# Transposes of keys, query and layer-norm output as interleaved 64-row halves in a decoder layer kernel

## The chip, the cores and the metric

The kernel runs on one core of one Trainium2 chip, in one launch. The metric is the device time of that launch in microseconds (us); lower is better.

## The reference: what is computed

One pre-norm decoder layer over 32 sequences of 128 tokens, width 512, all in fp32:

```
x = x + self_attention(layernorm(x))            # 16 heads of 32, rotary positions, causal
x = x + cross_attention(layernorm(x), ctx)      # 32 heads of 16, axial rotary positions; ctx is 128 x 256
x = x + ffn(layernorm(x))                       # gate and up 512 -> 1408, SiLU, down 1408 -> 512, integer weights
```

Only the two attentions are touched by the change. For each sequence they need queries, keys and values from the normalised input, and the heads' scores need queries and keys with the head dimension on the partitions, so each 128x512 query and key tile is transposed on TensorE before use. So are the normalised inputs (they are the stationary operand of the projections) and the softmax probabilities (they multiply the values).

## The kernel before, in words

Every engine has its own instruction stream, written out by hand, and they meet only in semaphores. The work is one loop over sequences, skewed: a call of `turn(sq, cq, nx, nz, oq)` does self-attention of sequence `sq`, cross-attention of `cq = sq - 1`, the first projections of `nx = sq + 1`, the layer norm of `nz = sq + 2` and the last projection of `oq = cq - 1`. `schedule` calls it for the first four turns with constants, then 27 times in a hardware loop, then once more; `last()` finishes the last sequences. In 30 of these turns both `sq` and `cq` exist. The feed-forward part follows. Each engine runs its part of `turn` in the order in which it is written; nothing else sets the order of the work.

There are eight PSUM banks: `S[0]` to `S[3]` hold scores and then the transposed probabilities; `PA`, `PB`, `PC` and `TC` serve all projections and transposes in rotation.

Names that the change and the prediction use:

- `transpose4` (L497) makes four 128x128 transposes of a 128x512 tile into one bank. It is used for the rotated query and key tiles (`rope_buf` in the profile: q1, k1 of self-attention, q2, k2 of cross-attention), for `z1` and `z2` (the two layer norms' outputs, `z` in the profile) and for the spread reciprocals (`rbc`).
- `transpose_prob` (L541 to L557) transposes 16 heads' probabilities as 32 transposes of 64 rows each. Rows 0 to 63 of one bank's heads alternate with rows 64 to 127 of another's, so two neighbours never write the same bank. The other halves follow after a wait on `cross_d`, which says that the first halves are complete. There are three such blocks in a turn: `"1"` for self-attention, `"2a"` and `"2b"` for the two halves of cross-attention.
- ScalarE copies the transposed query, keys and `z1` out of PSUM (`copy_q2`, `copy_q1`, `kT1` at L977, `z1T_high` at L867), ScalarE and VectorE share the copies of the transposed probabilities (`odd_copies` L936, `even_copies` L1105). Projections run in three passes of split operands, so VectorE also makes `z1T_l`, the remainder of `z1` (`z1T_low`, L1094).
- VectorE makes two products for each rotation (L1049, L1052), and GpSimd adds them (`rope_sum`, L399) into `RA[...]`; the semaphore `rot[...]` counts that.
- `normalise(1, ...)` on VectorE (L1028 to L1033) makes `z1` of `nz`.

In TensorE's `turn` the part that the change reaches is this, in order: project q2 and o2; transpose q2; `transpose_prob("1")`; values; scores 2a; attention 1; reciprocals; project q1 and o1; `transpose_prob("2a")`; transpose q1; keys k2; scores 2b; project k1; attention 2a; ten of twelve steps of v1 (L602); transpose k2; transpose k1; `transpose_prob("2b")`; the last two steps of v1; transpose z2; transpose z1 of `nz`; then the next turn's scores 1.

Of the kernel before, what the change touches and what calls it, by code (L numbers as in the profile page):

```python
# [15 lines left out]
P = 128  # L16
B = 32
# [121 lines left out]
def attention_phase(nc, fp32, fp32r, ALU, ACT, AX, x, ctx_in, pos, consts,  # L139
                    wq1, wk1, wv1, wo1, wq2, wkv2, wo2, bout, x2_dram, shared_f, shared, ident, mhalf_c, ffn):  # L140
    es = ExitStack()
    with es:
# [101 lines left out]
        cross_d = {n: sem(f"prob{n}T_first_quarters_done") for n in (1, 2)}  # L244
# [249 lines left out]
        def _(pe):  # L494
# [45 lines left out]

            def transpose_prob(u, q):  # L541
                k = kind(u)
                for swap in range(2):
                    for pair in range(2):
                        if swap == 0:
                            pe.wait_ge(p_r[k], G * nth(u, q) + 2 * pair + 2)
                        else:
                            pe.wait_ge(cross_d[k], 2 * nth(u, q) + pair + 1)
                        pe.sem_inc(gate, 1)
                        for i in range(G):  # L550
                            for half, rows in enumerate(HALVES):
                                c = 2 * pair + (half ^ swap)
                                last = nc.tensor.transpose(S[c][:, i * P + rows.start:i * P + rows.stop],  # L553
                                                           prob[rows, c, i, :], ident[rows, rows])
                        if swap == 0:
                            last.then_inc(cross_d[k], 1)
                        else:  # L557
                            last.then_inc(pT_d[k], 2)
# [33 lines left out]
            def transpose_z1(q, dst=PC):  # L592
                pe.wait_ge(z_r[1], q + 1)
                transpose4(dst, columns(z1)).then_inc(zT_d[1], 1)
# [17 lines left out]

            def project_k1(q):
                pe.wait_ge(rT_r["q1"], q + 1)
                project(PA, z1T_h, z1T_l, "k1", KT).then_inc(pj["k1"], 1)
# [12 lines left out]
            def turn(sq, cq, nx, nz, oq):  # L628
                has_s, has_c, has_n, has_o = sq is not None, cq is not None, nx is not None, oq is not None

                if is_first(nx):
                    first_projections()
                    return
# [20 lines left out]
                if has_c:  # L654
                    pe.wait_ge(zT_hi[2], cq + 1)
                    if has_n:
                        pe.wait_ge(zT_hi[1], nx + 1)
                        pe.wait_ge(zT_lo[1], nx + 1)
# [22 lines left out]
                if has_s:  # L681
                    pe.wait_ge(v1_r, sq + 1)
                    if is_first(sq):
                        pe.wait_ge(zT_hi[1], nx + 1)
                        pe.wait_ge(zT_lo[1], nx + 1)
# [16 lines left out]
                if has_n and has_c:  # L702
                    transpose_q1(nx)
# [10 lines left out]
                if has_c:  # L714
                    if has_o:
                        pe.wait_ge(x2_r, oq + 1)
# [6 lines left out]
                if has_s:  # L723
                    pe.wait_ge(rot["k2"], sq + 1)
                    if is_first(sq):
                        pe.wait_ge(riT_r[1], 1)
                    transpose4(TC, columns(RA["k2"])).then_inc(rT_d["k2"], 1)
                if has_n:
# [120 lines left out]

            pe.wait_ge(c_ready, 6)  # L850
            transpose_z1(0)
            schedule(turn, pe.Fori, last)
# [3 lines left out]
        def _(act):  # L856
# [8 lines left out]
            def z1T_high(q, src=PC):  # L865
# [847 lines left out]
```

## Time and profile before

| | us |
|---|---|
| three runs | 1692.16, 1687.82, 3995.81 (median 1692.16) |
| the profiled execution's own time | 1687.21 |
| its span | 1685.4 |
| TensorE busy | 1641.8 |
| VectorE busy | 1150.1 |
| ScalarE busy | 972.0 |
| GpSimd busy | 552.8 |
| one turn, from one transpose of q1 to the next | 35.15 |

The busy times are of one profiled execution, whose time is the second row. Engines overlap, so busy times don't add up; a busy TensorE counts a matmul that is under way even when its neighbour has begun, so how long a group takes is read from start to start of groups. "PE" is the matmul side of TensorE, "PEld" its weight loads. An arrow behind "idle before" names what ended the wait.

### The profile page before, as it was taken

The numbers are of one execution on the slowest core, as the hardware profiler recorded it, in microseconds if no ns is written. First come the engines' busy times: TensorE is split into PE (matmuls) and PEld (weight loads), VectorE is DVE, ScalarE is ACT, GpSimd is POOL, SyncE is SP. The second block draws the span as 40 slices with busy tenths as digits, with TensorE's granted clock in tenths as the row PEclk, the third lists the DMA queues.
The fourth block names the chain that finished last, engine by engine and source line by source line (L and its number), as shares of the span: only waits on it lengthen the run. The fifth ranks groups of instructions, "written<-read, shape, count | busy, mean of one in ns | idle before, by whom it ended". The sixth has DMA issues, their size and how long they took to land. (4 is left out here: it accounts for less than half of the span.)

```text
span 1685.4 us, 40585 instructions
## 1 busy us (share of the span) xinstructions
PE 1641.8 (97%) x14608; PEld 1285.4 (76%) x14608; DVE 1150.1 (68%) x2087; ACT 972.0 (58%) x3817; POOL 552.8 (33%) x535
## 2 busy tenths in 40 slices
PE   6899999999999999999999999998999999999997
PEld 4677777777777777777777777766888888888885
DVE  7777778777787777877778787777744344344332
ACT  6577777777777777777677776766522222222221
POOL 4444444444444444444444444431011011011011
PEclk9999999999999999999999999999999999999999
DMA  6011111101110011100111101021520120120110
GB/s 214 29 32 31 36 43 41 30 30 36 42 42 30 30 36 41 43 30 30 36 39 45 30 30 39 19 74 65 174 76 19 56 75 21 54 75 23 52 50 26
DMA packets 55097, 80.98 MB, mean 48 GB/s; under 512 B 4880, under 2 KB 25488, under 8 KB 55056
## 3 DMA queue, kind: packets, MB, share of 16 engines
q1 hardware_dynamic: 55056, 80.43, 14.6%
q8 instruction: 27, 0.44, 0.1%
q14 instruction: 14, 0.11, 0.0%
HBM read 63.63 MB, written 16.78 MB: 48 GB/s over the span
## 5 line engine op out<-in xcount | busy, mean ns | idle before, releaser
L877 ACT ACTIVATE prob<-bank,nmax 128x128 f32<-128x128 f32 x1536 | 541.3, 408 | 151.0 <-DVE nmax L1099 148.1
L877 ACT ACTIVATION_READ_ACCUMULATOR prob<-bank,nmax 128x1 f32 x1536 | 380.2, 248 | 0.0
L1099 DVE TENSOR_REDUCE nmax<-bank 128x4 f32<-128x512 f32 x376 | 233.5, 683 | 71.4 <-PE bank L536 70.7
L1505 PE MATMUL fbank<-shared,piece_hi 128*128 128x512 f32 x1152 | 280.3, 394 | 0.0
L1505 PEld LDWEIGHTS fbank<-shared,piece_hi 128*128 128x128 f32 x1152 | 215.8, 187 | 53.2
L399 POOL TENSOR_TENSOR rope_buf<-rope_buf 128x512 f32<-128x512 f32 x128 | 168.0, 1323 | 175.6 <-DVE rope_buf L1052 175.5
L1657 DVE SCALAR_TENSOR_TENSOR h<-fbank,su_c,sil 128x512 f32<-128x512 f32 x88 | 65.9, 749 | 198.4 <-PE fbank L1505 197.0
L1591 ACT ACTIVATE sil<-fbank,sg_c 128x512 f32<-128x512 f32 x88 | 60.6, 688 | 173.1 <-PE fbank L1505 172.0
L449 POOL TENSOR_TENSOR cn_l<-cn,cn_h 128x512 fp32r<-128x512 f32 x64 | 82.9, 1296 | 230.2 <-DVE cn L1091 230.2
L1597 ACT ACTIVATE h_h<-h 128x512 fp32r<-128x512 f32 x88 | 55.6, 632 | 175.0 <-DVE h L1657 175.0
L512 PE MATMUL bank<-shared,z1T_h 128*128 128x512 f32 x520 | 140.3, 411 | 4.3 <-ACT shared L860 2.6
L936 ACT ACTIVATE probT<-bank 128x512 f32<-128x512 f32 x186 | 101.1, 596 | 66.1 <-PE bank L553 66.1
L1105 DVE COPY probT<-bank 128x512 f32<-128x512 f32 x186 | 117.8, 675 | 29.2 <-PE bank L553 29.2
L1488 POOL TENSOR_TENSOR xr<-xr,ys 128x512 f32<-128x512 f32 x32 | 40.3, 1294 | 288.9 <-DVE ys L1677 288.9
L553 PEld LDWEIGHTS bank<-ident,prob 64*128 64x128 f32 x2976 | 111.7, 138 | 23.5 <-issue 22.4
L553 PE MATMUL bank<-ident,prob 64*128 64x64 f32 x2976 | 125.7, 229 | 0.5 <-ACT prob L877 0.5
L512 PEld LDWEIGHTS bank<-shared,z1T_h 128*128 128x128 f32 x520 | 93.7, 190 | 34.4 <-issue 12.9
L1520 PE MATMUL fbank<-piece_hi,h_h 128*128 128x512 f32 x288 | 115.3, 400 | 0.5 <-DVE h_l L1660 0.5
L1520 PE MATMUL fbank<-piece_hi,h_l 128*128 128x512 f32 x288 | 113.6, 395 | 0.0
L1660 DVE TENSOR_TENSOR h_l<-h,h_h 128x512 fp32r<-128x512 f32 x88 | 62.9, 714 | 61.5 <-ACT h_h L1597 61.5
L405 POOL TENSOR_TENSOR rbc<-rinv,one_c 128x512 f32<-128x512 f32 x64 | 66.6, 1041 | 76.7 <-DVE rinv L1114 56.6
L536 PE MATMUL bank<-kT,qT 32*128 32x256 f32 x1024 | 76.4, 404 | 5.1 <-DVE probT L1151 3.0
(171 smaller groups left out, 3127.4 us busy)
## 6 DMA issues: line engine op xcount, KB each, us to landing
xA<-in_x SPq DMA_DIRECT2D x32, 256.0 KB, 2.9
xB<-in_x SPq DMA_DIRECT2D x32, 256.0 KB, 2.8
x_scratch<-x SPq DMA_DIRECT2D x32, 256.0 KB, 2.0
shared_loaded<-x_scratch SPq DMA_DIRECT2D x8, 1024.0 KB, 7.8
xr<-x_scratch SPq DMA_DIRECT2D x8, 1024.0 KB, 5.6
out<-xr SPq DMA_DIRECT2D x8, 1024.0 KB, 4.3
cx<-in_ctx SPq DMA_DIRECT2D x32, 128.0 KB, 2.2
range_window<-in_wg SPq DMA_DIRECT2D x27, 112.0 KB, 2.0
```

Of the source, the lines that this page charges most:

```text
L399: pool.tensor_tensor(RA[n][:, :], RA[n][:, :], RB[n][:, :], ALU.add).then_inc(rot[n], 1)
L405: pool.tensor_tensor(tile[:, :, :], r[:, :].unsqueeze(2).to_broadcast([P, h, w]), one_c[:, :].unsqueeze(2).to_broadcast([P, h, w]), ALU.mu ...
L449: pool.tensor_tensor(cn_l[:, :, :], cn[:, :, :], cn_h[:, :, :], ALU.subtract).then_inc(cn_lo[n], 1)
L512: last = nc.tensor.matmul(dst[:, :], a[:, j, :], w[:, j, cols], start=(n == 0), stop=(n == 3 * k - 1))
L536: last = nc.tensor.matmul(S[g][:, 2 * P * i:2 * P * (i + 1)], qT2[rows, j, :], kT2[rows, j, :, :].rearrange("p e t -> p (e t)"), start=Tru ...
L553: last = nc.tensor.transpose(S[c][:, i * P + rows.start:i * P + rows.stop], prob[rows, c, i, :], ident[rows, rows])
L877: last = nc.scalar.activation(prob[:, c, i, :], S[c][:, i * P:(i + 1) * P], ACT.Exp, bias=nmax[:, c, i:i + 1], accum_out=rs[:, h:h + 1])
L936: nc.scalar.activation(probT[:, c, :, :].rearrange("p g t -> p (g t)"), S[c][:, :], ACT.Copy).then_inc(pTo_r[kind(u)], 1)
L1099: nc.vector.tensor_reduce(out=nmax[:, c, :], in_=S[c][:, :].rearrange("p (g k) -> p g k", g=G), op=ALU.max, axis=AX, negate=True).then_inc ...
L1105: nc.vector.tensor_copy(probT[:, c, :, :].rearrange("p g t -> p (g t)"), S[c][:, :]).then_inc(pTe_r[kind(u)], 1)
L1505: last = nc.tensor.matmul(dst[:, :], w[:, k, cols], z[:, k, :], start=(n == 0), stop=(n == len(passes) * KT - 1))
L1520: last = nc.tensor.matmul(DN[s][:, :], a[j % 2][:, tok], w[piece][:, j % 2, :], start=(j == 0 and n == 0), stop=(j == HT - 1 and n == len( ...
```

## The change: what it does

- **Keys.** k2 and k1 are transposed together as 64-row halves: rows 0 to 63 of k2 into `TC` alternate with rows 64 to 127 of k1 into `PA`; after that the first halves of the first two banks of `"2b"` probabilities; then, after a wait on the first halves of the keys, the other halves of both. The block waits for both `rot["k2"]` and `rot["k1"]` before it begins.
- **Second query and z1.** The transpose of the next input's `z1` leaves the end of the turn and is paired in the same way with q2, inside the block of `"1"` probabilities, one turn later in number (`nx` in place of `nz`). ScalarE's `z1T_high` moves behind `copy_q2`, VectorE's `z1T_low` moves behind `even_copies("1")`, and VectorE's `normalise(1, ...)`, which overwrites `z1`, moves behind the rotation of q1.
- **First query.** q1's two row halves go to two banks, 256 columns of `PA` and 256 of `PB`, as eight 64-row transposes with no second set; ScalarE copies it with two instructions of 128x256 in place of one of 128x512. The wait for `x2_r` (the residual sum that reads `PB`) comes forward with it.
- One semaphore, `halves_d`, replaces `cross_d`; a Python counter gives the value to wait for.

The core of the diff:

```diff
+            def halves_of_two(tiles, swap):
+                for j in range(KT):
+                    last = []
+                    for half, rows in enumerate(HALVES):
+                        dst, src = tiles[half ^ swap]
+                        last.append(nc.tensor.transpose(dst[:, j * P + rows.start:j * P + rows.stop],
+                                                        src[rows, j * P:(j + 1) * P], ident[rows, rows]))
+                return last
+            def transpose_keys_and_probs(sq, cq, nx):
+                keys = ((TC, RA["k2"]), (PA, RA["k1"]))
+                pe.wait_ge(rot["k2"], sq + 1)
...
+                pe.wait_ge(rot["k1"], nx + 1)
+                keys_ready = first_halves_of_two(keys)
+                if cq is not None:
+                    ready = [first_halves_of_probs("2b", cq, 0)]
+                k2, k1 = second_halves_of_two(keys, keys_ready)
...
+            def transpose_query_z1_and_probs(sq, cq, nx):
+                tiles = ((PA, RA["q2"]), (PC, z1))
+                pe.wait_ge(rot["q2"], cq + 1)
+                pe.wait_ge(v1_r, sq + 1)
+                pe.wait_ge(z_r[1], nx + 1)
+                tiles_ready = first_halves_of_two(tiles)
+                ready = [first_halves_of_probs("1", sq, 0)]
+                q2, z = second_halves_of_two(tiles, tiles_ready)
...
+            def transpose_q1_halves(q):
+                pe.wait_ge(rot["q1"], q + 1)
+                pe.sem_inc(gate, 1)
+                for j in range(KT):
+                    for half, rows in enumerate(HALVES):
+                        last = nc.tensor.transpose((PA, PB)[half][:, j * P // 2:(j + 1) * P // 2],
+                                                   RA["q1"][rows, j * P:(j + 1) * P], ident[rows, rows])
+                last.then_inc(rT_d["q1"], 1)
...
@@ turn of TensorE @@
-                    pe.wait_ge(rot["q2"], cq + 1)
-                    transpose4(PA, columns(RA["q2"])).then_inc(rT_d["q2"], 1)
-                if has_s:
+                    transpose_query_z1_and_probs(sq, cq, nx)
+                elif has_s:
                     transpose_prob("1", sq)
...
-                    transpose_q1(nx)
+                    if has_o:
+                        pe.wait_ge(x2_r, oq + 1)
+                    transpose_q1_halves(nx)
...
-                    pe.wait_ge(rot["k2"], sq + 1)
...
-                    transpose4(TC, columns(RA["k2"])).then_inc(rT_d["k2"], 1)
-                if has_n:
-                    pe.wait_ge(rot["k1"], nx + 1)
-                    transpose4(PA, columns(RA["k1"])).then_inc(rT_d["k1"], 1)
-                if has_c:
-                    transpose_prob("2b", cq)
+                    transpose_keys_and_probs(sq, cq, nx)
...
-                if nz is not None:
-                    pe.wait_ge(rT_r["k1"], nx + 1)
-                    transpose_z1(nz, PA)
```

TensorE at the keys, near the end of a turn, before (`rope_buf` is k2, then k1; `prob` is block "2b"; the first `z` is z2, the second z1):

```order
L602 MATMUL bank<-shared,z1T_l 128x512 x2
L497 MATMUL bank<-ident,rope_buf 128x128 x8
L553 MATMUL bank<-ident,prob 128x64 x32
L602 MATMUL bank<-shared,z1T_l 128x512 x2
L497 MATMUL bank<-ident,z 128x128 x8
L521 MATMUL bank<-causal,ident_b 32x512 x16
```

The first three of these rows in the changed kernel, with the waits (L578 is `halves_of_two`):

```order
L578 MATMUL bank<-ident,rope_buf 128x64 [waits rope_k2_ready,rope_k1_ready]
L578 MATMUL bank<-ident,rope_buf 128x64 x7
L553 MATMUL bank<-ident,prob 128x64 [waits prob2_ready]
L553 MATMUL bank<-ident,prob 128x64 x7
L578 MATMUL bank<-ident,rope_buf 128x64 [waits first_halves_transposed]
L578 MATMUL bank<-ident,rope_buf 128x64 x7
L553 MATMUL bank<-ident,prob 128x64 [waits prob2_ready]
L553 MATMUL bank<-ident,prob 128x64 x7
L553 MATMUL bank<-ident,prob 128x64 [waits first_halves_transposed]
L553 MATMUL bank<-ident,prob 128x64 x7
L553 MATMUL bank<-ident,prob 128x64 [waits first_halves_transposed]
L553 MATMUL bank<-ident,prob 128x64 x7
```

Eight full transposes became sixteen halves inside the block of probabilities. At q2 the pattern is the same, with q2 and `z1` in the places of k2 and k1 and block "1" in that of "2b"; behind z2, before L521, the four full transposes of `z1` are gone.

VectorE around `normalise(1, ...)` before, from the residual sum `x2` (written `x`) to the maxima of scores 2a:

```order
L1141 TENSOR_TENSOR x<-bank,x1B 128x512 [waits x1_bout_ready,proj_o2_done]
L1028 SCALAR_TENSOR_TENSOR nt<-r,ve 128x1 [waits rough_rstd1_ready]
L1030 TENSOR_SCALAR nt<-nt 128x1 [waits vector_small_step]
L1031 TENSOR_TENSOR nt<-nt,r 128x1 [waits vector_small_step]
L1033 TENSOR_SCALAR z<-xA,mv,nt 128x512 [waits z1T_done,vector_small_step]
L1114 RECIPROCAL rinv<-rsum 128x16 [waits rinv1_spread,prob1_ready]
L1105 COPY probT<-bank 128x512 [waits prob1T_done] x2
L1099 TENSOR_REDUCE nmax<-bank 128x4 [waits scores2_done] x4
```

VectorE in the changed kernel, from those copies of probabilities on (L1175 is `z1T_low`, L1130 and L1133 the rotation of q1, L1216 the residual sum `x1`):

```order
L1186 COPY probT<-bank 128x512 [waits prob1T_done] x2
L1175 TENSOR_TENSOR z1T_l<-bank,z1T_h 128x512 [waits z1T_hi_ready]
L1180 TENSOR_REDUCE nmax<-bank 128x4 [waits scores2_done] x4
L1171 TENSOR_TENSOR cn_h<-bank,rT 128x512 [waits attn_out1_done,rinv1T_ready]
L1172 TENSOR_TENSOR cn<-bank,rT 128x512
L1130 SCALAR_TENSOR_TENSOR rope_buf<-bank,cst 128x512 [waits rope_k2_ready,q1_transposed,proj_q1_done]
L1133 SCALAR_TENSOR_TENSOR rope_buf<-bank,cst 128x512
L1109 SCALAR_TENSOR_TENSOR nt<-r,ve 128x1 [waits rough_rstd1_ready]
L1111 TENSOR_SCALAR nt<-nt 128x1 [waits vector_small_step]
L1112 TENSOR_TENSOR nt<-nt,r 128x1 [waits vector_small_step]
L1114 TENSOR_SCALAR z<-xA,mv,nt 128x512 [waits z1T_done,vector_small_step]
L1216 TENSOR_TENSOR x1A<-bank,xB 128x512 [waits x1_bout_ready,x_residual_loaded,proj_o1_done]
```

The four instructions of `normalise(1, ...)` now stand between the rotation of q1 and the residual sum `x1` (in the hardware loop a reduction of feed-forward weights' range, L1272 of before, stands just ahead of them), and `z1T_l` between the copies of probabilities and the maxima.

## Rows read from the trace of the kernel before

**Rows 1.** The page: span, and busy time of the engines.

```profile
span 1685.4 us, 40585 instructions
PE 1641.8 (97%) x14608; PEld 1285.4 (76%) x14608; DVE 1150.1 (68%) x2087; ACT 972.0 (58%) x3817; POOL 552.8 (33%) x535
```

**Rows 2.** Stages: 50 to 1190 us, engines' busy us and counts, then clock.

```profile
50.00:1190.00 1140.00, 1126.05 (x12251) 870.12 (x12250) 901.30 (x1661) 810.89 (x3556) 485.86 (x468) 1.00 0.13 41
```

**Rows 3.** Timeline of TensorE's matmuls in one turn: start, us, instruction, count.

```profile
602.53 0.66 PE L497 MATMUL bank<-ident,rope_buf 128*128 128x128 f32 x4
...
612.04 1.03 PE L497 MATMUL bank<-ident,rope_buf 128*128 128x128 f32 x8
613.00 1.37 PE L553 MATMUL bank<-ident,prob 64*128 64x64 f32 x32
614.30 0.73 PE L602 MATMUL bank<-shared,z1T_l 128*128 128x512 f32 x2
614.87 1.03 PE L497 MATMUL bank<-ident,z 128*128 128x128 f32 x8
615.83 0.43 PE L521 MATMUL bank<-causal,ident_b 32*32 32x512 bf16 x16
...
624.63 0.66 PE L497 MATMUL bank<-ident,rope_buf 128*128 128x128 f32 x4
...
626.48 0.73 PE L512 MATMUL bank<-w_kv_hi,cxT_h 128*128 128x512 f32 x2
...
628.08 1.15 PE L536 MATMUL bank<-kT,qT 32*128 32x256 f32 x16
...
637.68 0.66 PE L497 MATMUL bank<-ident,rope_buf 128*128 128x128 f32 x4
638.09 0.71 PE L512 MATMUL bank<-w_kv_hi,cxT_h 128*128 128x512 f32 x2
```

**Rows 4.** Timeline of TensorE's matmuls, from 613.0 to 613.5 alone.

```profile
613.00 0.71 PE L553 MATMUL bank<-ident,prob 64*128 64x64 f32 x16
```

**Rows 5.** Timeline of TensorE's matmuls, from 613.0 to 613.7 alone.

```profile
613.00 0.89 PE L553 MATMUL bank<-ident,prob 64*128 64x64 f32 x18
```

**Rows 6.** Weight loads of transposes by form: count, busy us, mean ns, idle before.

```profile
L553 PEld LDWEIGHTS bank<-ident,prob 64*128 64x128 f32 x2976 | 111.7, 138 | 23.5 <-issue 22.4
L497 PEld LDWEIGHTS bank<-ident,rope_buf 128*128 128x128 f32 x512 | 56.7, 140 | 20.9 <-POOL rope_buf L399 14.5
```

**Rows 7.** Timeline of GpSimd: the sums of k2 and k1.

```profile
609.49 2.54 POOL L399 TENSOR_TENSOR rope_buf<-rope_buf 128x512 f32<-128x512 f32 x2 [4.10 <-DVE rope_buf L1052]
```

**Rows 8.** Timeline of VectorE in the same turn, with idle time before.

```profile
611.02 1.02 DVE L1031 TENSOR_TENSOR nt<-nt,r 128x1 f32<-128x1 f32 x1
...
612.67 0.69 DVE L1297 COPY rope_buf<-bank 128x512 f32<-128x512 f32 x1
614.12 1.29 DVE L1105 COPY probT<-bank 128x512 f32<-128x512 f32 x2 [0.76 <-PE bank L553]
...
625.46 0.21 DVE L1028 SCALAR_TENSOR_TENSOR nt<-r,ve 128x1 f32<-128x1 f32 x1
...
626.18 0.55 DVE L1033 TENSOR_SCALAR z<-xA,mv,nt 128x512 f32<-128x512 f32 x1
...
634.87 0.84 DVE L1272 TENSOR_REDUCE range_per_window<-range_window 128x672 int32 x1
636.64 0.69 DVE L1135 TENSOR_TENSOR x1A<-bank,xB 128x512 f32<-128x512 f32 x1 [0.93 <-PE bank L512]
...
640.88 2.48 DVE L1099 TENSOR_REDUCE nmax<-bank 128x4 f32<-128x512 f32 x4 [0.97 <-PE bank L536]
```

**Rows 9.** Timeline of ScalarE in the same turn, with idle time before.

```profile
616.00 0.59 ACT L867 ACTIVATE z1T_h<-bank 128x512 fp32r<-128x512 f32 x1
...
625.33 0.60 ACT L893 ACTIVATE qT<-bank 128x512 f32<-128x512 f32 x1 [0.97 <-PE bank L497]
626.33 1.09 ACT L936 ACTIVATE probT<-bank 128x512 f32<-128x512 f32 x2 [0.41 <-PE bank L553]
```

More of the change, by code:

```diff
@@ L539, in scores2 @@
                 last.then_inc(s_done[2], 1)
-            def transpose_prob(u, q):
-                k = kind(u)
-                for swap in range(2):
-                    for pair in range(2):
[L545 to L558, printed above, removed]
+            crossed = {"n": 0, "base": 0}
@@ new lines, in first_halves_end, with halves_of_probs @@
+            def first_halves_end(last):
+                last.then_inc(halves_d, 1)
+                crossed["n"] += 1
+                return crossed["base"] + crossed["n"]
+            def halves_of_probs(u, pair, swap):
+                for i in range(G):
+                    for half, rows in enumerate(HALVES):
+                        c = 2 * pair + (half ^ swap)
+                        last = nc.tensor.transpose(S[c][:, i * P + rows.start:i * P + rows.stop],
+                                                   prob[rows, c, i, :], ident[rows, rows])
+                return last
@@ new lines, in halves_of_two, with first_halves_of_two @@
+            def halves_of_two(tiles, swap):
[5 more added lines that the diff above has]
+                                                        src[rows, j * P:(j + 1) * P], ident[rows, rows]))
+                return last
+            def first_halves_of_two(tiles):
+                pe.sem_inc(gate, 1)
+                return first_halves_end(halves_of_two(tiles, 0)[1])
@@ new lines, in second_halves_of_two @@
+            def second_halves_of_two(tiles, ready):
+                pe.wait_ge(halves_d, ready)
+                pe.sem_inc(gate, 1)
+                second, first = halves_of_two(tiles, 1)
+                return first, second
+            def transpose_keys_and_probs(sq, cq, nx):
+                keys = ((TC, RA["k2"]), (PA, RA["k1"]))
+                pe.wait_ge(rot["k2"], sq + 1)
+                if is_first(sq):
+                    pe.wait_ge(riT_r[1], 1)
+                pe.wait_ge(rot["k1"], nx + 1)
[3 more added lines that the diff above has]
+                k2, k1 = second_halves_of_two(keys, keys_ready)
+                k2.then_inc(rT_d["k2"], 1)
+                k1.then_inc(rT_d["k1"], 1)
+                if cq is not None:
+                    ready.append(first_halves_of_probs("2b", cq, 1))
+                    for pair in range(2):
+                        second_halves_of_probs("2b", pair, ready[pair])
@@ L848, in transpose_ffn_head, with turns_of @@
                     last.then_inc(f_zT, 1)
+            LOOP_HALVES = 8
+            before = {"n": 0}
+            @contextmanager
+            def turns_of(a, b):
+                before["n"] = crossed["n"]
+                with pe.Fori(a, b) as c:
+                    yield c
             pe.wait_ge(c_ready, 6)
             transpose_z1(0)
-            schedule(turn, pe.Fori, last)
+            schedule(turn, turns_of, last)
         @block.scalar
@@ L965, in turn @@
                     odd_copies("2a", cq)
[L966 removed]
+                if is_first(nx):
                     copy_q1(nx)
+                if has_n and has_c:
+                    copy_q1_halves(nx)
                 if is_first(sq):
@@ L1255, in turn @@
                     add_cross(oq)
-                if nz is not None:
+                if nz is not None and not has_c:
                     normalise(1, xA, z1, nz)
@@ L1273, in turn @@
                                             op=ALU.max, axis=AX, apply_absolute_value=True).then_inc(rng_r, 1)
+                if nz is not None and has_c:
+                    normalise(1, xA, z1, nz)
                 if is_first(sq):
```

64 lines of the change are left out of this document (42 added, 22 removed).

## The prediction

> **What bounds the kernel now.** I read the page first: the span is 1685.4 us and TensorE is busy for 1641.8 of them [rows 1]. In the stretch from 50 to 1190 us, which holds the loop of turns, it is busy 1126.05 of 1140.00 us at the full granted clock, VectorE 901.30 and ScalarE 810.89 [rows 2]. The reader is to see that the loop is TensorE's: a turn is as long as its matmuls and transposes from start to start. The timeline of TensorE gives the turn: from one transpose of q1 to the next 637.68 - 602.53 = 35.15 us [rows 3]. Whatever the change takes out of TensorE's stream comes off the time, unless an engine that now has slack becomes late. So two questions remain: how long the transposes take in either form, and how much slack each moved piece has.
>
> **Price of a transpose in each form.** Eight full transposes last 1.03 us from the first's start to the last's end; the last counts 0.27, so the step is (1.03 - 0.27)/7 = 0.109 us [rows 3]. Of a block of 32 halves, the first 16 last 0.71 us with the last at 0.22 or a little over: a step of 0.49/15 = 0.033 us [rows 4]. A full transpose is two halves, 0.066 us, so the form saves 0.043 each. The weight load of a half is as long as a full one's (138 against 140 ns, [rows 6]); the halves are cheap only because two neighbours use different rows and run side by side.
>
> Three fixed costs come with blocks of halves.
> - Entering: eight full transposes from 612.04, yet the halves start at 613.00, which is 0.96 - 8 x 0.109 = 0.09 more than the steps [rows 3].
> - Second halves: the 17th half is the first that waits for a completion, that of the eighth. The 16th starts at 613.49; the 18th ends at 613.89 [rows 4, 5], so with a duration of 0.22 to 0.27 it starts at 613.62 to 613.67, where two steps would give 613.56. I take a gap of 0.10 before the 17th, which then starts near 613.61. The eighth starts at 613.00 + 7 x 0.033 = 613.23: from the start of the last first half to the restart is 0.38 us, and eight other halves in between cover most of it.
> - Leaving: the whole block is 614.30 - 613.00 = 1.30, against 32 x 0.033 + 0.10 = 1.16, so 0.14 for the way back and for group boundaries [rows 3].
>
> **The change, part by part.**
> - *Keys.* Before, from k2's first transpose to the last two steps of v1: 614.30 - 612.04 = 2.26 us [rows 3]. After: entering 0.09, 48 halves x 0.033 = 1.58, the gap before the keys' second halves 0.10, a second gap before the last set, which now also has only eight halves between itself and its first halves, 0.38 - 9 x 0.033 = 0.08, and leaving 0.14. Sum 1.99, gain 0.27. The block now waits for k1 before k2 starts. GpSimd ends k1's sum at 609.49 + 2.54 = 612.03 [rows 7], and TensorE arrives at 612.04. Before, k1 was wanted only four transposes later, at 612.04 + 4 x 0.109 = 612.48; that slack is now nil. From semaphore to first transpose I take 0.05 beyond what entering costs anyway (bounds 0 and 0.13, the latter the wait after a completion above). Gain 0.22.
> - *q2 with z1.* Before: 626.48 - 624.63 = 1.85, plus z1's four in the end of the turn, 4 x 0.109 = 0.43; 2.28 in all [rows 3]. After: the same 1.99 as the keys. Gain 0.29; I take 0.27, since q2's sum is also just in time there and the entry is the same. z1's wait at its old place is gone and z1 is long made at the new one.
> - *q1.* Before: 638.09 - 637.68 = 0.41 [rows 3]. After: eight halves, 0.26, in the row mode that the block before it has left on, with no second set. Gain 0.15. ScalarE pays one more instruction; the copy is wanted only by project k1, behind the keys projection and scores 2b, over 2.5 us later. The wait for `x2_r` is for a sum made 12 us before.
> - *What the moved copies push.* With U the start of the q2 block: q2's and z1's second halves complete near U + 1.15, and ScalarE then copies q2, z1, and two banks. One such copy costs about 0.49 in a row (1.09 for two, 0.60 the last, [rows 9]): 1.2 + 3 x 0.49 + 0.6 = U + 3.3. Scores 2a want those banks at U + 1.99 + 1.60 = U + 3.6 (1.60 is 628.08 - 626.48, [rows 3]). Slack 0.3, cost nothing; if it is gone, scores 2a wait. VectorE's `z1T_l` fits before attention 1, which wants it after another 1.1.
> - *End of the turn.* The next scores 1 want the copied banks of block "2b". TensorE reaches them at 612.04 + 1.99 + 0.57 (two steps of v1, 614.87 - 614.30) + 0.43 (z2) + 0.2 = 615.23. VectorE copies k2 at about 613.25 once its halves are complete, then two banks, 0.69 and 1.29 [rows 8]: 613.25 + 0.69 + 1.21 = 615.15. These meet within 0.1. Cost 0, bounds 0 and 0.3.
> - *`normalise(1)`.* It took 626.18 + 0.55 - 625.46 = 1.27 us. In its new place VectorE has 0.93 idle before the residual sum and another 0.97 before the maxima of scores 2b [rows 8], so it is late by 0.34 at the first and back in time at the second. Cost 0.
>
> **A rule against a row.** In rows, a step of two side-by-side halves is 0.066 us, less than one full transpose. The Trainium skill, "TensorE: Matmul & The Clock Gate", section "LDWEIGHTS (loading the stationary operand)", says that a weight load costs its columns at 1.2 GHz whatever its rows: 107 ns for either form. By that a pair of halves costs as much as one full transpose, and the change would gain nothing. The trace agrees with the page on the full form (0.109) and on equal loads for both forms, and not on the pair's step.
> A second row matters for `normalise(1)` in its new place: the third step of `normalise(2)`, one column wide, takes 1.02 us while GpSimd adds k1 [rows 7, 8]. The Trainium skill, "SBUF — State Buffer", section "SBUF: two separate sides", says that VectorE and GpSimd share a port pair as an exclusive lock, held for a whole instruction; by it the step would wait for the end of GpSimd's sum, and the trace agrees: 611.02 + 1.02 = 612.04 against 612.03. What that would do at the new place is worked out from the row, in the first rival.
>
> **Sum.** 0.22 + 0.27 + 0.15 = 0.64 us per turn. There are 30 turns with all three; the first turn's keys are in halves with nothing between the sets, worth 0.1 once and left out. 30 x 0.64 = 19. Against the profiled execution's own 1687.2 that is 1668. The median of the runs shown is 5.0 higher, the lowest run 0.6 higher; I stay with the sum.
>
> **Rivals.**
> - *The waits eat part of it.* The keys' gate (0.13), the banks at the end of the turn (0.3), or VectorE: if `normalise(1)` is stretched by GpSimd's q1 sum as the third step above was (1.02 where its neighbours take 0.2, so 0.8 more), VectorE is 0.34 + 0.8 = 1.1 late at the residual sum and 0.2 to 0.3 late at the maxima, and k1's gate passes that on. Any one leaves 0.3 to 0.5 a turn: 30 times that off 1687 is 1672 to 1678. For it: three chains come in within 0.1 to 0.3. Against: GpSimd's sum of q1 follows the rotation directly, and the range reduction of 0.84 us [rows 8] covers most of it.
> - *No gain.* In the new pairs a pair's step equals a full one's, 0.109. Then nothing is saved by the form and the fixed costs remain, two second gaps of 0.08 and the gate of 0.05, so 0.2 a turn is lost: 1687 to 1693. Against it: the step of 0.033 in [rows 4]. This is where the page's rule on weight loads leads.
> - *Slower.* Halves from two tiles, or into two half banks, do not run side by side at all: 40 halves at the full step of 0.109 replace 20 full ones, +2.2 a turn and 0.2 of fixed costs: 30 x 2.4 = 72, 1759. It decides from a step of (20 x 0.109 - 0.2)/40 = 0.050 up. Against it: the probabilities' neighbours already differ in bank and rows, as the new pairs do, and keep 0.033 [rows 4].
> - *More.* The gaps are covered better, 20 x 0.043 = 0.86 a turn: 1661, and as much as 1658 if entry is cheaper too.
>
> **Chances.** Forecast (gain of 0.5 to 0.8 a turn, 1663 to 1672) 0.68; waits eat part 0.17; more 0.08; no gain 0.04; slower 0.03. The range runs from 1659 to 1681: it takes in the forecast, most of both neighbours and the run-to-run spread. Of this kernel's measurement about 2% (34 us of 1692) can be told from no change. Over 2% faster would need under 1658, half of the "more" case at best and a draw of runs: 0.06. Slower over 2% is the slower rival: 0.03. The same: 0.91.
>
> **What would show it.** After the change, a turn of about 34.5 us from q1 to q1. The keys block from its first half to v1's last steps about 2.0; the q2 block to the values projection about 2.0; q1's eight halves to the keys projection 0.25 to 0.3. No idle time of TensorE before scores 1, scores 2a or scores 2b put down to copies. The halves' first step 0.033, also with z1 in the pair. VectorE's idle before the maxima of scores 2b down from 0.97 but not gone. I am wrong if the turn is shorter by under 0.5 or the row steps differ between tiles; then the step to look at is the gate on k1 first, the banks before scores 1 second.

## The result, and the profile after

| | before | after |
|---|---|---|
| median of the runs, us | 1690.01 | 1679.31 |
| profiled execution's own time, us | 1687.21 | 1680.36 |
| its span, us | 1685.4 | 1678.5 |
| mean turn, scores 1 to scores 1, us | 35.148 | 34.750 |

The ratio of the times is 0.9934 [0.992, 0.9949]: about 11 us faster, within 2% of no change, and inside the range. The forecast was 1668: about 19 us were expected. One of the five runs of before took 3995.81 us; it counts in the median and not in the ratio. Turns here and below are means over 24 turns of one profiled execution, each from the first matmul of scores 1 (L521) to the next. Moving the 24 turns one later changes no mean by more than 0.01; the first turns are left out, since in some of the kernels below one of them is 1 to 3 us longer. They carry the argument, because 0.40 us less a turn is 30 x 0.398 = 11.9 us, and the two profiled executions differ by only 6.9. The rest is in the clock outside the hardware loop. The stages from 20 to 60 and from 1095 to 1150 us, first before, then after (columns as in [rows 2]; the column behind POOL is the granted clock):

```profile
20.00:60.00 40.00, 32.40 (x280) 24.40 (x279) 32.52 (x52) 22.18 (x66) 17.04 (x14) 0.96 0.23 77
...
1095.00:1150.00 55.00, 49.95 (x531) 37.52 (x529) 43.02 (x87) 39.52 (x174) 19.09 (x18) 0.97 0.18 59
```

```profile
20.00:60.00 40.00, 32.14 (x277) 23.44 (x276) 31.31 (x50) 19.93 (x55) 17.04 (x14) 0.91 0.23 77
...
1095.00:1150.00 55.00, 48.47 (x523) 36.71 (x524) 43.63 (x87) 40.28 (x180) 17.20 (x16) 0.91 0.17 54
```

The granted clock has the two levels 1.2 and 2.4 GHz here, so a mean of 0.91 over 55 us is 9.9 us at the lower one, 0.97 is 3.3; in the first stage it is 7.2 against 3.2. Together 10.6 more us at half speed, worth up to 5.3. TensorE has idle time in both stages (32.14 of 40.00 us busy, 48.47 of 55.00), while from 60 to 1095 us, in the loop, it is busy for 1021.89 of 1035.00 at the full clock (before 1031.91, the same clock). The stretches change from run to run: the five runs of after go from 1675.96 at a mean clock of 0.997 to 1680.36 at 0.993.

The page of after, which answers to [rows 1]:

```profile
span 1678.5 us, 42062 instructions
PE 1625.0 (97%) x15216; PEld 1267.4 (76%) x15216; DVE 1162.9 (69%) x2087; ACT 967.3 (58%) x3847; POOL 548.4 (33%) x535
```

TensorE has 608 matmuls more and 16.8 us less busy time. Its timeline in the turn that answers to [rows 3]:

```profile
608.07 0.63 PE L666 MATMUL bank<-shared,z1T_l 128*128 128x512 f32 x2
608.63 0.46 PE L578 MATMUL bank<-ident,rope_buf 64*128 64x64 f32 x8
...
609.53 1.08 PE L553 MATMUL bank<-ident,prob 64*128 64x64 f32 x24
610.53 0.73 PE L666 MATMUL bank<-shared,z1T_l 128*128 128x512 f32 x2
611.10 0.60 PE L497 MATMUL bank<-ident,z 128*128 128x128 f32 x4
611.89 0.44 PE L521 MATMUL bank<-causal,ident_b 32*32 32x512 bf16 x16 [0.19 <-DVE probT L1186]
...
619.67 1.10 PE L512 MATMUL bank<-w_o_hi,cn_l 128*128 128x512 f32 x4
620.88 0.24 PE L578 MATMUL bank<-ident,rope_buf 64*128 64x64 f32 x1
...
620.97 0.22 PE L578 MATMUL bank<-ident,rope_buf 64*128 64x64 f32 x1
621.00 0.22 PE L578 MATMUL bank<-ident,z 64*128 64x64 f32 x1
...
622.75 0.73 PE L512 MATMUL bank<-w_kv_hi,cxT_h 128*128 128x512 f32 x2
...
623.78 0.63 PE L512 MATMUL bank<-w_kv_hi,cxT_l 128*128 128x512 f32 x2
624.34 1.15 PE L536 MATMUL bank<-kT,qT 32*128 32x256 f32 x16
...
632.65 1.33 PE L553 MATMUL bank<-ident,prob 64*128 64x64 f32 x32
633.79 0.44 PE L682 MATMUL bank<-ident,rope_buf 64*128 64x64 f32 x8
634.16 0.73 PE L512 MATMUL bank<-w_kv_hi,cxT_h 128*128 128x512 f32 x2
```

The rows of before that show where it came to the same blocks: the v1 steps ahead of the keys, the last pass of o2, and block "2a":

```profile
611.57 0.62 PE L602 MATMUL bank<-shared,z1T_l 128*128 128x512 f32 x2
...
623.63 1.09 PE L512 MATMUL bank<-w_o_hi,cn_l 128*128 128x512 f32 x4
...
636.38 1.37 PE L553 MATMUL bank<-ident,prob 64*128 64x64 f32 x32
```

From group to group these rows and [rows 3] give where the turn changed:

| stretch of TensorE | before | after | gain |
|---|---|---|---|
| v1's split steps to v1's last steps (keys, "2b") | 2.73 | 2.46 | 0.27 |
| v1's last steps to scores 1 (z2, before also z1) | 1.53 | 1.36 | 0.17 |
| last pass of o2 to the values (q2, after also z1, "1") | 2.85 | 3.08 | -0.23 |
| block "2a" to the keys projection (q1) | 1.71 | 1.51 | 0.20 |

The sum is 0.41, against 0.398 by the means. The reader is to see two things. At the end of the turn z1's four transposes, 0.43 of work, are gone, yet only 0.17 came off, and an idle time stands before scores 1 that was not there. And inside the q2 block the first half starts 1.21 behind the last pass of o2, where the full transpose before started after 1.00.

The rows of VectorE and GpSimd that those starts wait for:

```profile
609.76 0.69 DVE L1382 COPY rope_buf<-bank 128x512 f32<-128x512 f32 x1 [0.63 <-PE bank L578]
610.37 1.28 DVE L1186 COPY probT<-bank 128x512 f32<-128x512 f32 x2
```

```profile
605.99 2.53 POOL L399 TENSOR_TENSOR rope_buf<-rope_buf 128x512 f32<-128x512 f32 x2 [3.59 <-DVE rope_buf L1133]
...
619.36 1.28 POOL L399 TENSOR_TENSOR rope_buf<-rope_buf 128x512 f32<-128x512 f32 x1 [0.34 <-DVE rope_buf L1133]
```

VectorE's copies end at 611.65; scores 1 start 0.24 later. GpSimd's sum of q2 ends at 620.64; the first half starts 0.24 later. The trace also has the records of TensorE's sequencer (waits, register work, weight loads), which the views above leave out; these are their starts:

| | released by, ends | wait | next wait | weight load | matmul |
|---|---|---|---|---|---|
| after, scores 1 | copy, 611.65 | 611.683 | 611.780 | 611.856 | 611.887 |
| after, first half of q2 | sum, 620.64 | 620.685 | 620.777 | 620.854 | 620.885 |
| before, q2 | sum, 624.58 | in the load | none | 624.629 | 624.632 |

A wait that stands on an instruction of its own passes 0.03 to 0.05 after its releaser. Each instruction behind it on the sequencer adds 0.08 to 0.10; here that is `pe.sem_inc(gate, 1)`, which stands ahead of the block and carries the remaining waits. From the releaser's end to the first matmul there are thus three distances, and each repeats over at least 20 turns within about 0.01:

- 0.05 where the wait is on the weight load itself (q2 in before and in `keys_only`);
- 0.10 where it is on the `sem_inc` directly ahead (the keys behind k1's sum in after; q2 in `keys_q1_q2half` below);
- 0.24 where that `sem_inc` still follows (scores 1 and q2 in after).

The forecast lacked the third.

### The profile page after: what moved, and what is told of

Same layout as the page of the kernel before. It is cut to its first block and busy times, and to the rows that moved or that the text cites. A ratio compares the mean times of both kernels' runs of the same rounds, so it can differ in the third digit from the quotient of the medians.

```text
span 1678.5 us, 42062 instructions
## 1 busy us (share of the span) xinstructions
PE 1625.0 (97%) x15216; PEld 1267.4 (76%) x15216; DVE 1162.9 (69%) x2087; ACT 967.3 (58%) x3847; POOL 548.4 (33%) x535
## 5 line engine op out<-in xcount | busy, mean ns | idle before, releaser
L553 PE MATMUL bank<-ident,prob 64*128 64x64 f32 x2976 | 133.8, 226 | 0.4 <-ACT prob L949 0.4
L553 PEld LDWEIGHTS bank<-ident,prob 64*128 64x128 f32 x2976 | 117.6, 138 | 13.3 <-issue 12.3
L421 POOL TENSOR_TENSOR kT<-rope_buf,cst 128x512 f32<-128x512 f32 x62 | 63.2, 1040 | 62.7 <-DVE rope_buf L1382 62.7
```

## The experiments

All times are against the kernel before, whose median is that of the same group of runs. Each kernel of this section ran five times, `q2z1_only` eleven and `all_orders_split9` four times. Every one of these kernels computes the whole layer. The ratios are known to about 0.0015, 2.5 us, so they separate only the larger steps: after and `after_probsfirst` have nearly the same ratio (0.9934 and 0.9933), though their turns differ by 0.132. Comparisons below therefore go by the turn, with one profiled execution for each kernel, and 0.01 a turn is no difference.

| run | median, us | before, us | ratio | turn | against |
|---|---|---|---|---|---|
| keys_only | 1680.17 | 1688.94 | 0.9945 [0.9931, 0.9958] | 34.842 | before -0.306 |
| q1_only | 1681.04 | 1688.94 | 0.996 [0.9946, 0.9975] | 34.962 | before -0.186 |
| q2z1_only | 1689.43 | 1688.94 | 1.0005 [0.9996, 1.0015] | 35.166 | before +0.018 |
| keys_q1 | 1677.23 | 1688.94 | 0.9927 [0.9913, 0.9941] | 34.690 | before -0.458 |
| after_cover | 1682.38 | 1689.16 | 0.9957 [0.9943, 0.997] | 34.913 | after +0.163 |
| after_split9 | 1679.9 | 1689.16 | 0.9938 [0.9925, 0.9952] | 34.739 | after -0.011 |
| after_z2pa | 1676.65 | 1689.16 | 0.9926 [0.9912, 0.994] | 34.646 | after -0.104 |
| after_probsfirst | 1678.63 | 1689.16 | 0.9933 [0.9919, 0.9947] | 34.618 | after -0.132 |
| z2pa_probsfirst | 1674.3 | 1690.13 | 0.9912 [0.9898, 0.9926] | 34.528 | after -0.222 |
| all_orders | 1675.26 | 1690.13 | 0.9918 [0.9905, 0.9932] | 34.568 | z2pa_probsfirst +0.040 |
| all_orders_split9 | 1668.9 | 1690.13 | 0.9876 [0.9861, 0.9892] | 34.350 | all_orders -0.218 |
| keys_q1_q2half | 1677.35 | 1690.13 | 0.9934 [0.992, 0.9947] | 34.685 | keys_q1 -0.005 |

**Each part alone.** `keys_only` is before with this part:

```diff
-                    transpose4(TC, columns(RA["k2"])).then_inc(rT_d["k2"], 1)
...
-                    transpose4(PA, columns(RA["k1"])).then_inc(rT_d["k1"], 1)
...
-                    transpose_prob("2b", cq)
+                    transpose_keys_and_probs(sq, cq, nx)
```

> Only the keys in pairs of halves; q2, z1 and q1 as before. Theory (z1's four transposes at the end of the turn covered VectorE's copies, and leave a wait when they go): here they stay, the keys' block is 0.27 us shorter and nothing waits, 30 x 0.27 = 8 us less than before. Rival (the keys' gate on k1 costs part of the gain, and the loss is spread over all parts): 30 x 0.13 = 4 us less.

`q1_only` is before with `transpose_q1_halves` and ScalarE's two copies:

```diff
-                    transpose_q1(nx)
+                    if has_o:
+                        pe.wait_ge(x2_r, oq + 1)
+                    transpose_q1_halves(nx)
```

> Only q1 as halves into two half banks. Both theories: block of probabilities to the keys projection shorter by 0.15 to 0.20 us in every turn, 30 x 0.2 = 6 us less than before by the trace of the changed kernel, 4.5 by the prediction. The rival on spread losses: 3 us.

`q2z1_only` is before with q2 and z1 as a pair, and the moves on ScalarE and VectorE that go with it:

```diff
-                    transpose4(PA, columns(RA["q2"])).then_inc(rT_d["q2"], 1)
...
-                    transpose_prob("1", sq)
+                    transpose_query_z1_and_probs(sq, cq, nx)
...
-                    transpose_z1(nz, PA)
```

> Only q2 paired with z1, with z1's copies and its normalisation moved. Theory: z1's 0.43 us at the end of the turn turn into a wait of about 0.2 to 0.25 before scores 1, the q2 block is 0.23 longer, so 0 gain: 0 to 2 us more than before. Rival (this part gives its share of the prediction): 30 x 0.17 to 0.27 = 5 to 8 us less.

`keys_q1` is the changed kernel without that pair: q2 in full transposes, z1 at the end of the turn.

> The changed kernel without the pair of q2 and z1. Theory: 30 x (0.27 + 0.20) = 14 us less than before, so 3 us less than the changed kernel. Rival (spread losses): 7 us less than before, 4 us more than the changed kernel.

The keys and q1 carry the whole gain; q2 with z1 is worth nothing, with an interval of [0.9996, 1.0015]. With keys and q1 already in, adding the pair makes a turn 0.060 longer; that is 1.8 us over 30 turns, where 3 were expected, and `keys_q1` stands 13.7 us below before by its turn and 11.7 by the medians, for 14 expected. The single gains add up to 0.492, more than the 0.458 of both: in each single run a block of probabilities that the run leaves alone is 0.03 shorter too (means from block "2a" to the keys projection: 1.71 in before, 1.68 in `keys_only`). Why is not known. So of the forecast's three terms the keys came out above their 0.22, q1 above its 0.15, and q2 with z1 at about zero instead of 0.27.

**Is there an idle time before scores 1?** `after_cover` puts 0.43 us of transposes there whose result nobody uses:

```diff
                     transpose4(TC, columns(z2)).then_inc(zT_d[2], 1)
+                if has_s and nz is not None:
+                    pe.wait_ge(rT_r["k1"], nx + 1)
+                    pe.wait_ge(z_r[1], nz + 1)
+                    transpose4(PA, columns(z1))
```

> The changed kernel with four full transposes of z1 into PA put back behind z2's in each turn, their result unused. Theory (scores 1 wait about 0.26 us for VectorE's copies): 0.43 us of work fills that wait and costs only 0.17 to 0.2 a turn, 30 x 0.18 = 5 to 6 us more than the changed kernel. Rival (no wait worth the name there): 30 x 0.43 = 13 us more.

The turn grew by 0.163, 4.9 us over 30 turns: 0.27 of the 0.43 was idle time already paid for. The rows with it:

```profile
612.34 1.03 PE L497 MATMUL bank<-ident,z 128*128 128x128 f32 x8
613.30 0.43 PE L521 MATMUL bank<-causal,ident_b 32*32 32x512 bf16 x16
```

Eight transposes take the 0.96 that they took before, and no wait is left.

**Is k1's sum what the keys' block waits for?** `after_split9` moves one step of v1 behind the block:

```diff
-            V1_SPLIT = 10
+            V1_SPLIT = 9
```

> The changed kernel with nine steps of v1 ahead of the keys' block and three behind, in place of ten and two. Theory (k1's sum arrives as TensorE does, so the block can't start earlier, and scores 1 hang on the copies that follow the block): the same time as the changed kernel within 1 us; the wait before scores 1 turns into a wait before the keys. Rival (only the wait before scores 1 counts, the keys could start earlier): 0.23 of cover, 30 x 0.23 = 7 us less.

There is no change, as expected if the wait for k1's sum (the gate on k1) holds the block back. The waits from 500 to 1000 us (us in total, times, longest), first in after, then in this kernel:

```profile
PEld bank L578 <- issue: 12.9, 29, 0.5
```

```profile
PEld bank L578 <- issue: 15.9, 29, 0.6
```

Of the 29 blocks 15 or 14 are keys; 3.0 over those is 0.2 a block, the length of the step. TensorE came earlier and waited for it. In after, the sum ends at 605.99 + 2.53 = 608.52, and the block starts 0.11 later; over 20 turns the distance is 0.10 to 0.11 in both kernels. TensorE's own way into the block costs 0.09 anyway, so in after TensorE and the sum meet.

**Copies before scores 1.** `after_z2pa` has z2 transposed into `PA`, so that VectorE can copy the probabilities first and k2 afterwards:

```diff
-                    pe.wait_ge(k2T_c, sq + 1)
-                    transpose4(TC, columns(z2)).then_inc(zT_d[2], 1)
+                    pe.wait_ge(rT_r["k1"], nx + 1)
+                    transpose4(PA, columns(z2)).then_inc(zT_d[2], 1)
...
@@ VectorE: even_copies("2b") ahead of the copy of k2; GpSimd: spread(2) ahead of key_pairs @@
```

> The changed kernel with z2 transposed into PA in place of TC, so that VectorE can copy the two banks of probabilities ahead of k2 (and GpSimd spreads the reciprocals ahead of the key pairs). Theory (VectorE's copy of k2, 0.6 us, stands ahead of the copies that scores 1 wait for): the wait of 0.26 goes, 30 x 0.2 to 0.26 = 6 to 8 us less than the changed kernel. Rival (the wait is for something else, or moves to z2's copies or to the reciprocals): 0 to 2 us less.

This expectation missed: the turn is 0.104 shorter, against 0.2 to 0.26. VectorE, then TensorE:

```profile
642.42 1.29 DVE L1191 COPY probT<-bank 128x512 f32<-128x512 f32 x2 [1.12 <-PE bank L553]
```

```profile
640.80 0.46 PE L578 MATMUL bank<-ident,rope_buf 64*128 64x64 f32 x8
...
643.95 0.44 PE L521 MATMUL bank<-causal,ident_b 32*32 32x512 bf16 x16
```

The copies begin 1.62 behind the block's first half; in after, behind k2's copy, they begin 610.37 - 608.63 = 1.74 behind it. k2's copy had held them up by only 0.12, because they wait for TensorE's own second halves (the row names `PE bank L553`). They end at 643.71, and scores 1 start 0.24 later once more. So do they in `q2z1_only`, `after_split9`, `after_probsfirst` and `z2pa_probsfirst` (means 0.24 to 0.25), all without z1's transposes ahead of them.

**The gate on q2.** `after_probsfirst` puts the first probabilities ahead of the wait:

```diff
                 tiles = ((PA, RA["q2"]), (PC, z1))
+                ready = [first_halves_of_probs("1", sq, 0)]
                 pe.wait_ge(rot["q2"], cq + 1)
...
                 tiles_ready = first_halves_of_two(tiles)
-                ready = [first_halves_of_probs("1", sq, 0)]
+                ready.append(first_halves_of_probs("1", sq, 1))
                 q2, z = second_halves_of_two(tiles, tiles_ready)
```

> The changed kernel with the first eight halves of block 1 ahead of q2's and z1's. Theory (the q2 block starts 0.2 us after TensorE is free because it waits for GpSimd's sum of q2 on TensorE's sequencer, and the last gap goes): 0.1 to 0.17 a turn, 3 to 5 us less than the changed kernel, unless scores 2a begin to wait for ScalarE's copies. Rival (entering costs this much anyway): no change or 1 us more.

0.132 came back, inside what was expected. `z2pa_probsfirst` joins it with the run before:

> The changed kernel with both reorderings: z2 into PA with the probabilities' copies first, and block 1's first eight halves ahead of q2 and z1. By turn length (34.750 us in the changed kernel, 0.104 less with the one, 0.132 less with the other): if the two waits are separate, 34.51 us, 27 to 30 turns x 0.24 = 7 us less than the changed kernel; if they hang on the same chain, 34.6.

0.222 against 0.104 + 0.132: the two repairs lie at two places and add up. Its q2 block shows a third chain coming in:

```profile
617.56 1.10 PE L512 MATMUL bank<-w_o_hi,cn_l 128*128 128x512 f32 x4
...
620.34 0.73 PE L512 MATMUL bank<-w_kv_hi,cxT_h 128*128 128x512 f32 x2
...
621.38 0.63 PE L512 MATMUL bank<-w_kv_hi,cxT_l 128*128 128x512 f32 x2
622.12 1.15 PE L536 MATMUL bank<-kT,qT 32*128 32x256 f32 x16
```

From o2's last pass to the values it is 2.78, 0.30 less than in after. But scores 2a start 0.74 behind the third pass of the values, where the pace, the distance when nothing waits, is 0.56 (before, 628.08 - 627.52): 0.18 is given back there. `after_probsfirst` has the same block; ScalarE in it:

```profile
624.19 1.09 ACT L1014 ACTIVATE probT<-bank 128x512 f32<-128x512 f32 x2
```

These copies end at 625.28, the weight load of scores 2a follows at 625.35 and the first matmul at 625.38, later than VectorE's copies (624.76). They are the copies for which the prediction had a slack of 0.3: in after they end at 624.07, 0.27 ahead of scores 2a, and this order uses that up.

**Probabilities first in the keys' block too.** `all_orders` also starts the keys' block with probabilities and has ScalarE copy a bank of them ahead of k1:

```diff
+                    probs_ready = first_halves_of_probs("2b", cq, 0)
                 keys_ready = first_halves_of_two(keys)
...
+                if has_c:
+                    odd_copies("2b", cq, (1,))
@@ ScalarE: copy of k1, then odd_copies("2b", cq, (3,)) @@
```

> The same, and in the keys' block the probabilities' first eight halves ahead of the keys and their second halves ahead of the keys' second halves; ScalarE copies bank 1 ahead of k1. Theory (scores 1 wait for the copies, which wait for the transposes of the first two banks): these come 0.3 us earlier, the wait of 0.18 before scores 1 and one gap of 0.1 go, a turn of 34.3 us. Rival (the keys' completion is then late for z2 and PA): 34.5 or more.

`all_orders_split9` is the same with one v1 step more behind the block (`V1_SPLIT = 9`):

> The same with nine steps of v1 ahead of the keys' block and three behind. If something is still waited for behind the block, up to 0.23 a turn less than with ten; if not, no change; if k1's gate now bites, up to 0.1 more.

The first expectation missed: a turn of 34.57 against 34.3, which its rival (34.5 or more) had. The second kernel gained 0.218 where the same edit had gained 0.011 in after. TensorE and ScalarE in `all_orders`:

```profile
606.24 0.46 PE L553 MATMUL bank<-ident,prob 64*128 64x64 f32 x8
...
608.11 0.73 PE L667 MATMUL bank<-shared,z1T_l 128*128 128x512 f32 x2
608.68 0.60 PE L497 MATMUL bank<-ident,z 128*128 128x128 f32 x4
609.46 0.44 PE L521 MATMUL bank<-causal,ident_b 32*32 32x512 bf16 x16 [0.17 <-issue]
```

```profile
607.85 0.59 ACT L1066 ACTIVATE kT<-bank 128x512 f32<-128x512 f32 x1
608.33 0.60 ACT L1020 ACTIVATE probT<-bank 128x512 f32<-128x512 f32 x1
```

The last copy of probabilities ends at 608.93, so by the 0.24 scores 1 could start at 609.17. They start at 609.46, and the row says "issue": nothing outside TensorE. The sequencer's records have it. k1's copy ends at 608.44; the wait for it ahead of z2 passes at 608.49; then come the end of the loop's turn, a branch at 608.74 with register work at 609.01, and the waits of the next turn at 609.14, 609.25 and 609.35; the matmul starts at 609.457, 0.717 behind the branch. In all 23 turns whose branch lies between 200 and 1000 us the distance from branch to matmul is 0.716 or 0.717. In `z2pa_probsfirst` it is 1.21 to 1.23, and in after 1.15 to 1.18: there it isn't what the matmul waits for. As long as k1's copy is early, the sequencer runs through all this under the matmuls that are still queued. This order had moved k1's copy 0.49 back, behind a bank of probabilities, and so laid it open. The block itself gained nothing by the new order: 1.87 from its first half to v1's last steps, as with the keys first (608.49 - 606.62 in `z2pa_probsfirst`). With a v1 step more behind the block:

```profile
604.77 0.47 PE L553 MATMUL bank<-ident,prob 64*128 64x64 f32 x8
...
607.45 0.60 PE L497 MATMUL bank<-ident,z 128*128 128x128 f32 x4
608.00 0.44 PE L521 MATMUL bank<-causal,ident_b 32*32 32x512 bf16 x16
```

z2 to scores 1 is 0.55, the pace, and scores 1 stand 3.23 behind the block's first half as they did without the step (609.46 - 606.24 = 3.22). The 0.23 of the step filled the wait, and the branch is now 0.72 to 0.77 ahead of the matmul. That the branch is what lay open is read from the records and agrees with this run; a kernel with k1's copy first and all else the same was not run. This is the best version: 1668.9 us, ratio 0.9876 [0.9861, 0.9892].

**Another form for q2.** `keys_q1_q2half` gives q2 the form of q1, eight halves into two half banks, with z1 left at the end:

```diff
-                    transpose4(PA, columns(RA["q2"])).then_inc(rT_d["q2"], 1)
+                    pe.sem_inc(gate, 1)
+                    for j in range(KT):
+                        for half, rows in enumerate(HALVES):
+                            last_q2 = nc.tensor.transpose((PA, PC)[half][:, j * P // 2:(j + 1) * P // 2],
+                                                          RA["q2"][rows, j * P:(j + 1) * P], ident[rows, rows])
```

> Keys in pairs and q1 in half banks as in the run without the q2 and z1 pair (turn 34.690 us), and q2 also as eight halves into half of PA and half of PC, with no second set. By the form alone 0.17 to 0.19 a turn less, as q1 gave: 34.50. If the wait for GpSimd's sum of q2, now on TensorE's sequencer and not on the weight load, costs what it did in the changed kernel (first half 0.24 us after the sum, against 0.05), 0.15 of it is lost again: 34.65.

The form gained nothing here: 34.685 against 34.690. TensorE, then VectorE:

```profile
619.49 1.10 PE L512 MATMUL bank<-w_o_hi,cn_l 128*128 128x512 f32 x4
...
622.11 0.72 PE L512 MATMUL bank<-w_kv_hi,cxT_h 128*128 128x512 f32 x2
...
623.95 1.15 PE L536 MATMUL bank<-kT,qT 32*128 32x256 f32 x16 [0.19 <-DVE probT L1202]
```

```profile
622.05 0.55 DVE L1130 TENSOR_SCALAR z<-xA,mv,nt 128x512 f32<-128x512 f32 x1
...
622.68 1.22 DVE L1202 COPY probT<-bank 128x512 f32<-128x512 f32 x2
```

The form gave its 0.23 (2.62 for 2.85), and scores 2a gave it back (1.84 behind the values, against 1.60 in [rows 3]). VectorE's copies end at 623.90, 4.41 behind the last pass of o2. `normalise(1)` in its old place stands ahead of them. These copies had set scores 2a in the kernel before already, with nothing to spare: they end 628.03 - 623.63 = 4.40 behind the same pass there, and scores 2a start at 628.08.

```profile
626.81 1.22 DVE L1105 COPY probT<-bank 128x512 f32<-128x512 f32 x2
```

The expectation's 34.65 came near, but for the wrong reason. It had put the loss at the gate on q2, with 0.24; that gate took 0.10 (GpSimd's sum ends at 620.47, the first half starts at 620.58). The loss is at the copies. This form with `normalise(1)` moved, as in the changed kernel, was not run.

## Why the prediction was partly right

- **The form's price** was right. The halves step by 0.03 also between two tiles (q2's half at 620.97, z1's at 621.00), and q1's eight into two half banks last no longer (0.44) than eight of keys (0.46). "No gain" and "slower" fell with it: `keys_only` and `q1_only` gained 0.306 and 0.186 a turn. The Trainium skill, "TensorE: Matmul & The Clock Gate", section "LDWEIGHTS (loading the stationary operand)", says that a weight load's time goes by its columns and not by its rows. The trace agrees for one load (138 ns for a half, 140 for a full one, [rows 6]). That a pair of halves would then cost a full transpose was the prediction's own step, and the trace refutes it: two loads of different rows overlap.
- **Keys** (0.22 predicted): 0.27 on the timeline. The block lasts 1.90 from its first half, which is the predicted 1.99 less the 0.09 for entering. The 0.05 for the gate on k1 was not needed: TensorE enters while it waits.
- **q1** (0.15): 0.20. The first half starts 1.14 behind the first of block "2a" (633.79 - 632.65), where the full transpose started after 1.30 ([rows 3] and the row of block "2a"), and 0.37 later the keys projection follows, where 0.26 was meant. What the prediction calls leaving is paid once, behind q1.
- **End of the turn** (cost 0, bounds 0 and 0.3): this step failed. It compared TensorE's arrival, 615.23, with the end of the last copy, 615.15, and called them level. The copies ended 3.13 behind k1's sum, as forecast (615.15 - 612.03 = 3.12), but the two sequencer instructions and the weight load behind them are 0.24 more, as six kernels show, and `after_cover` priced the idle time (0.27). The cost was 0.26 a turn, inside the bounds and nearer the upper one.
- **q2 with z1** (0.27): this step failed too. "The entry is the same" was wrong: the old wait was carried by the weight load (0.05 behind the sum), the new one stands ahead of another wait (0.24). Of that difference of 0.19 the sum already had 0.09 as entering, and from its first half the block took 1.87 instead of 1.90. So the stretch grew by 0.23 where 0.16 was meant. Together with the idle time at the end of the turn nothing is left of the pair, as `q2z1_only` shows.
- **`normalise(1)`** (cost 0) was right, and its rival's mechanism is there to see. The Trainium skill, "SBUF — State Buffer", section "SBUF: two separate sides", calls the port of VectorE and GpSimd an exclusive lock; the trace agrees: the first step, 0.21 in [rows 8], takes 0.71 and ends at 597.88, GpSimd's sum of q1 at 597.87. It cost no time of TensorE:

```profile
597.17 0.71 DVE L1109 SCALAR_TENSOR_TENSOR nt<-r,ve 128x1 f32<-128x1 f32 x1
...
602.23 2.48 DVE L1180 TENSOR_REDUCE nmax<-bank 128x4 f32<-128x512 f32 x4 [0.46 <-PE bank L536]
```

```profile
596.58 1.29 POOL L399 TENSOR_TENSOR rope_buf<-rope_buf 128x512 f32<-128x512 f32 x1 [0.33 <-DVE rope_buf L1133]
```

- **ScalarE's copies before scores 2a** (cost 0) were judged rightly: 624.34 - 623.78 = 0.56, the pace.

In sum: 0.64 + 0.05 (keys) + 0.05 (q1) - 0.26 (end of turn) - 0.07 (q2 block) = 0.41 a turn, 12 us instead of 19. By the prediction's own sign, a turn shorter by under 0.5, its forecast was wrong: 0.40 came. It had named the banks before scores 1 as the second step to look at; the first it named, the gate on k1, cost nothing, and the wait before q2 it did not name. What happened is the rival "the waits eat part of it" (0.3 to 0.5 a turn, 1672 to 1678, chance 0.17), by the second of its three waits. The time fell inside the range because the range took in that rival: the median of 1679.31 is 1.3 above the rival's upper edge and 1.7 below the end of the range, and the clock outside the loop, which no term of the sum was about, moves single runs by more than that.

## What to carry to other kernels

A wait does not end when its producer does: add what the waiting engine still has to issue behind it, and put the wait whose producer is last directly on the instruction that needs it, with the other waits ahead. Work removed just ahead of such a wait pays only down to the arrival of the next chain; ask which chain comes next and by how much, and leave independent work (here one step of a projection) behind the block to fill the difference, where the block itself can then start earlier. Where an engine loops, keep its last early wait well ahead of the branch, so that the branch runs under queued work. No run here moved a wait or the branch alone; these two pieces of advice are worked out from the distances 0.05, 0.10, 0.24 and 0.717.

## What the runs showed of the hardware

- From the branch of TensorE's hardware loop, through the register work and the three waits behind it, to the first matmul it was 0.717 us in each of 23 turns of `all_orders`, which cost 0.2 to 0.3 a turn because a late wait stood ahead of the branch. In after, where the branch came 1.15 to 1.18 ahead, it cost nothing.
- From a producer's end to the first matmul that waits for it: 0.05 us with the wait on the weight load, 0.10 with it on a sequencer instruction directly ahead, 0.24 with one more sequencer instruction between.
- Halves of 64 rows that alternate between two row halves stepped by 0.03 us each, also between two tiles and into two half banks, with weight loads of 138 ns that overlap; full transposes stepped by 0.109.
- The block of sixteen halves of keys and 32 of probabilities took 1.87 us with the keys first and 1.87 with probabilities first (`z2pa_probsfirst` and `all_orders`): where the sets stand in it made no difference.
- With 16.8 us less work TensorE kept the full clock in its loop. The stretches at 1.2 GHz lay outside it, 17.1 us in the two stages above against 6.5 before, and the time of a run went up as its mean clock went down.
